# Half-width streams in the doubling of a delta rule's inverse

## The reference, cut to what matters

```python
def step(S, inp):
    q_t, k_t, v_t, g_t, b_t = inp
    Sk = jnp.einsum('bhkv,bhk->bhv', S, k_t)
    delta = jnp.einsum('bhv,bhk->bhkv', v_t, k_t) - jnp.einsum('bhv,bhk->bhkv', Sk, k_t)
    S = jnp.exp(g_t)[..., None, None] * S + b_t[..., None, None] * delta
    o_t = jnp.einsum('bhkv,bhk->bhv', S, q_t)
    return (S, o_t)
_, o = jax.lax.scan(step, S0, xs)
```

## Time and profile before

| | us |
|---|---|
| median of 3 runs | 5181.56 |
| lowest and highest | 5180.79, 5186.57 |
| the profiled execution | 5157.29 |
| span of its trace, first to last instruction | 5155.5 |

### The profile page before, as it was taken

One profiled execution on the slowest core, in us unless ns is written; L12 is line 12 of the kernel. 1 busy time (PEld: TensorE's weight loads), 2 busy tenths in 40 slices (PEclk: granted clock), 3 DMA queues, 4 the chain that ended last, 5 costly groups with the idle time before them and its releaser, 6 DMA issues. The chain is left out here.

```text
span 5155.5 us, 162507 instructions
## 1 busy us (share of the span) xinstructions
PE 4638.3 (90%) x67085; PEld 2981.7 (58%) x67085; DVE 3206.6 (62%) x5639; ACT 2103.2 (41%) x2965; POOL 1162.3 (23%) x1361
## 2 busy tenths in 40 slices
PE   6877869999999999999976666999999999999998
PEld 6333349999999999997644443344444444444443
DVE  4888864444444444443334445787877878787876
ACT  1566632222222222221332221565655656565654
POOL 1355533232323232321014445000000000000000
PEclk9989989999999999999987776999999999999999
DMA  3322221111111111112232224000000000000000
GB/s 103 132 98 98 91 100 51 54 51 54 51 54 46 58 45 60 42 53 63 77 116 63 60 63 99 8 9 12 9 12 8 14 17 4 17 4 17 10 12 8
DMA packets 201355, 250.09 MB, mean 49 GB/s; under 512 B 52865, under 2 KB 132865, under 8 KB 199969
## 3 DMA queue, kind: packets, MB, share of 16 engines
q1 hardware_dynamic: 180240, 209.29, 13.0%
q0 software_dynamic: 6144, 16.79, 1.1%
q10 hardware_dynamic: 14352, 14.55, 0.8%
HBM read 135.18 MB, written 105.38 MB: 47 GB/s over the span
## 5 line engine op out<-in xcount | busy, mean ns | idle before, releaser
L2096 DVE TENSOR_REDUCE part_max<-p_m 128x1 f32<-128x512 f32 x2118 | 1364.0, 686 | 379.6 <-PE p_m L1938 372.1
L2078 ACT ACTIVATE prob<-p_s 128x1024 f32<-128x1024 f32 x1024 | 1047.7, 1023 | 750.4 <-PE p_s L2002 748.5
L1957 PE MATMUL p_o<-prob,v_one 128*64 128x512 f32 x4096 | 1054.3, 592 | 3.9 <-ACT prob L2078 0.5
L1938 PE MATMUL p_m<-keys,queries 96*64 96x512 f16 x4236 | 661.5, 387 | 27.5 <-DMA keys<-parts_d 19.9
L2002 PE MATMUL p_s<-queries,keys 97*64 97x512 f16 x4096 | 619.2, 380 | 1.2 <-issue 0.6
L2002 PEld LDWEIGHTS p_s<-queries,keys 97*64 97x64 f16 x4096 | 227.9, 109 | 600.7 <-issue 594.3
L544 PE MATMUL p_proj<-xn_t_all,proj_w_sb 128*128 (+1 forms) x768 | 389.2, 649 | 78.7 <-ACT raw L570 70.5
L1050 DVE TENSOR_TENSOR inv<-inv,pd_pre 128x512 f32<-128x512 f32 x256 | 176.1, 688 | 406.7 <-PE pd_pre L795 406.7
L962 ACT ACTIVATE inv_low<-pd_low 128x512 f32<-128x512 f32 x320 | 191.0, 597 | 579.4 <-PE pd_low L833 528.3
L1938 PEld LDWEIGHTS p_m<-keys,queries 96*64 96x64 f16 x4236 | 239.3, 108 | 310.5 <-DVE part_max L2096 56.4
L1906 POOL TENSOR_TENSOR attn<-o_num,o_inv 32x512 f32<-32x512 f32 x64 | 81.0, 1265 | 1452.5 <-DVE o_inv L2115 1446.1
(11 more groups left out here) (240 smaller groups left out, 6624.5 us busy)
## 6 DMA issues: line engine op xcount, KB each, us to landing
k_d<-qkv SPq DMA_DIRECT2D x8, 2048.0 KB, 7.5
q_d<-qkv SPq DMA_DIRECT2D x8, 2048.0 KB, 12.3
v_d<-qkv SPq DMA_DIRECT2D x8, 2048.0 KB, 7.3
sums<-sums_d SPq DMA_DIRECT2D x128, 128.0 KB, 3.0
k_t<-k_d SPq DMA_DIRECT2D x64, 256.0 KB, 3.3
q_t<-q_d SPq DMA_DIRECT2D x64, 256.0 KB, 3.4
v_t<-v_d SPq DMA_DIRECT2D x64, 256.0 KB, 4.8
slots_d<-zero ACTq DMA_DIRECT2D x1, 10112.0 KB, 31.9
```

The costliest lines, as they stand in the source:

```text
L1938: last = te.matmul(p_m[k % 2][x * HALF:(x + 1) * HALF, :], queries[0:ROW, p, hh, at:at + HALF], keys[0:ROW, 2 * p + hh, kb * BLK:(kb + 1) ...
L1957: product = te.matmul(p_o[64 * hh:64 * hh + VW, :], g.v_one[:, j, p, hh:hh + 2, :].rearrange("p a d -> p (a d)"), prob[:, j % 2, hh, :], s ...
L2078: a.activation(prob[:, j % 2], p_s[j % 2][:], ACT.Exp, scale=SCORE_SCALE).then_inc(exp_d, 1)
L2096: v.tensor_reduce(part_max[:, hh * SUB + sub, kb:kb + 1], p_m[k % 2][:], AX.X, ALU.max).then_inc(red_d, 1)
```

## The change

In levels 1 to 4 a matrix that is block diagonal with blocks of width 2w is made out of one with blocks of width w. Of the columns of a head only half can change: in `p_low` and `inv_low` the first w of each 2w, in `inv` the second w of each 2w. The changed kernel streams only these 32 of the 64 columns of a head, as a strided view with runs of w = 2, 4, 8 and 16 columns at k = 1 to 4 (at k = 5, for `half`, one run of 32):

```diff
+    def firsts(ap, k):
+        return ap.rearrange("q n (b s w) -> q n b s w", s=2, w=1 << k)[:, :, :, 0, :]
+    def seconds(ap, k):
+        return ap.rearrange("q n (b s w) -> q n b s w", s=2, w=1 << k)[:, :, :, 1, :]
+    def of_head(part, buffer, hs, p, k):
+        return part(buffer[hs, p:p + 1, :], k).rearrange("q n b w -> q (n b) w")
         def half(n, x, k):
-            each(p_pre[x], of(upper[x]), of(inv_low[x])).then_inc(half_d[x], 1)
+            for p, hs in heads():
+                last = te.matmul(of_head(firsts, p_pre[x], hs, p, k), upper[x][hs, p, :], of_head(firsts, inv_low[x], hs, p, k), start=True, stop=True)
+            last.then_inc(half_d[x], 1)
         def low(n, x, k):
-                last = te.matmul(p_low[x][hs, p, :], inv[x][hs, p, :], step[x][hs, p, :], start=False, stop=k == NL - 1, skip_group_check=True)
+                last = te.matmul(of_head(firsts, p_low[x], hs, p, k), inv[x][hs, p, :], of_head(firsts, step[x], hs, p, k),
+                                 start=False, stop=k == NL - 1, skip_group_check=True)
         def up(n, x, k):
             if k == NL:
                 wait_apart(pe, g, (step_d[x], n.level[k]))
-            each(p_pre[x], of(step[x]), of(inv[x])).then_inc(upmm_d[x], 1)
+                last = each(p_pre[x], of(step[x]), of(inv[x]))
+            else:
+                for p, hs in heads():
+                    last = te.matmul(of_head(seconds, p_pre[x], hs, p, k), step[x][hs, p, :], of_head(seconds, inv[x], hs, p, k),
+                                     start=True, stop=True)
+            last.then_inc(upmm_d[x], 1)
         def keep_low(n, x, k):
-            a.activation(inv_low[x][:], p_low[x][:], ACT.Copy).then_inc(lowc_d[x], 1)
+            if k == 0:
+                a.activation(inv_low[x][:], p_low[x][:], ACT.Copy).then_inc(lowc_d[x], 1)
+            else:
+                a.activation(firsts(inv_low[x][:], k), firsts(p_low[x][:], k), ACT.Copy).then_inc(lowc_d[x], 1)
         def add_up(n, x, k):
-            v.tensor_tensor(inv[x][:] if k < NL else inv_fin[:, n.ring[x]], inv[x][:], p_pre[x][:], ALU.add).then_inc(up_d[x], 1)
+            if k < NL:
+                v.tensor_tensor(seconds(inv[x][:], k), seconds(inv[x][:], k), seconds(p_pre[x][:], k), ALU.add).then_inc(up_d[x], 1)
+            else:
+                v.tensor_tensor(inv_fin[:, n.ring[x]], inv[x][:], p_pre[x][:], ALU.add).then_inc(up_d[x], 1)
```

## The result

| | before | after |
|---|---|---|
| median, us (4 runs each) | 5182.28 | 5267.10 |
| lowest and highest | 5180.79, 5186.57 | 5228.49, 5275.96 |
| the profiled execution | 5157.29 | 5266.16 |
| its span and mean granted clock | 5155.5, 0.951 | 5264.4, 0.929 |

The changed kernel is slower: the ratio is 1.0148, its 95% interval 1.0097 to 1.0198. The forecast was faster, 5148 us. The time lies inside the range of 5065 to 5290, on the side of its rivals.

The account below looks back on a forecast made before the run. TensorE's stream, paced by 64-column weight loads, was taken to bound the delta phase. 832 groups x 0.04 us gave 33 us off 5157.3, 5124 us profiled; scaled to the runs 5148 us, range 5065 to 5290.

Parts of the forecast that it names:

- The pace of a group: TensorE, delta phase: loads of 64 columns set each group's step, with matmuls no longer than the load lying beside them.
- The naive 389 us: TensorE's 832 changed groups: saving of 0.47 us each if streamed columns set the pace; chance 0.06.
- The gain of 33 us: TensorE's 832 changed groups: 0.04 us off each, from 0.935 to 0.895 us.
- The 0.08 us between 0.855 and 0.935: A group's excess over half its lower-clock time; it might stay (0 us) or go entirely (67 us over 832 groups).
- main case's upper end: Delta phase load-bound with full clock, chance 0.58, between -67 and 0 us; at this end nothing is gained.
- ScalarE and VectorE at nothing: `keep_low` and `add_up`: 55 us less ScalarE and 70 us less VectorE work, costed at zero under TensorE's stream.
- The clock stays, 0.58: TensorE's granted clock stays full through the load-bound delta phase; chance 0.58, around -33 us.
- The rival, held at 0.20: TensorE's clock falls in the delta phase, 0.8 us per slow group; one in five gives 5282 us; chance 0.20.
- The strided stream, 0.12: Strided reads and PSUM writes slow changed groups: 82 us slower if only runs of two, 350 if all; chance 0.12.
- The floor per matmul, 0.04: A minimum time per matmul limits changed groups: from 0.935 to 0.80 us, 112 us gained, 5070 us; chance 0.04.
- TensorE's own stream alone bounds the phase, the stops are fixed: Delta phase as long as TensorE's stream; mid-group stops mostly unchanged, perhaps taking a third of the 33 us.
- The phase's end at 2384 us: The delta phase was taken to run from 728 to 2384 us.

Follow-up runs that it names:

- e_cols48: The changed kernel with the first 48 columns of a head streamed contiguously in the changed groups, not computing the inverse; ratio 0.9990.
- e_half_only: The changed kernel with `low` and `up` back at 64 streamed columns, only `half` streaming 32; ratio 0.9996.
- e1_engines_only: The kernel before with only the narrowed `keep_low` and `add_up` on ScalarE and VectorE, TensorE's products untouched; ratio 0.9991.
- e_last_both: Kernel before with narrowed ScalarE and VectorE work, level 5 of `half` and `up` at 32 loaded and streamed columns, `add_up` there split; ratio 1.0192.
- e_cols32: The changed kernel with the first 32 columns of a head streamed contiguously instead of the strided view, not computing the inverse; ratio 1.0201.
- e_both32: The changed kernel with 32 loaded and 32 contiguous streamed columns in the changed groups, not computing the inverse; ratio 0.9981.

## Why the prediction was wrong

**The pace of a group: right.** "With 64 columns of weights the load sets the step." 16, 32, 48 and 64 streamed columns give 0.93 us, 32 loaded columns give 0.89 and 0.52. The naive 389 us did not come. The steps of 0.107 and 0.105 us, read at the lower level in two different phases, had pointed to it.

**The gain of 33 us: over-sized, by the term of 0.04 us a group.** The 0.08 us between 0.855 and 0.935 stayed nearly whole; the group measures 0.93. It is the main case's upper end, "they stay: 0 us". In e_cols48 and e_half_only, where the clock holds, the gain is 0.1% and 0.04%, neither clear of zero. By the medians after is 85 us slower, less than the 110 us that its clock costs. Of the 25 us between, 12 are stops with no releaser: 60 us in the phase of after, 72 in that of e1_engines_only. A slow stretch takes fewer instructions in the same time and can make up for them. Whether the rest is a part of the gain is open.

**ScalarE and VectorE at nothing: right**, by e1_engines_only.

**The clock stays, 0.58: this step failed.** The rival, held at 0.20, came, and its price of 0.8 us a group measures 1.71 - 0.93 = 0.78. That 5267 us lies so near its 5282 is luck in part: it took one group in five, 166, at the lower level and 33 us of gain, and no row said how many. The 242 us more at that level are the time of 142 groups, and the gain didn't come. The arguments for it were in the rows already: a busy TensorE at the lower level with 16 streamed columns. What I held against it was that the clock had never fallen with the stops in the phase, and that 22 of 48 groups and `project` stay full. The first says nothing about narrow groups, since it was seen with full ones. The second is an average over a couple, where the narrow groups lie together; e_half_only, where they don't, keeps its clock. The Trainium skill ("TensorE: Matmul & The Clock Gate", section "HAM oscillation — how this bites in real kernels") tells of the clock falling where TensorE idles while it waits for data. The falls of e_last_both agree with it. The rows of after show the clock fall with TensorE busy for 7.37 of 8 us and never idle for more than 0.63, so that reading for idle gaps alone would have missed it.

**The strided stream, 0.12: refuted.** e_cols32 without stride is no faster than after, and runs of 2 to 16 columns leave a group at 0.93. The rule of the Trainium skill that any non-contiguous pattern in PSUM slows matmuls ("Advanced Engine Details and Errata", section PSUM Cachelines) is not seen here, at least not behind loads of this length; whether it would be in a group bound by its stream no run tested.

**The floor per matmul, 0.04: refuted.** Cut to 16 columns the group keeps its 0.93, and in e_both32 32 records take 0.52 us, 16 ns apart on average. That is below the 25 ns that the Trainium skill states ("TensorE: Matmul & The Clock Gate", section "Wait — 56ns, not 53.3ns?"). The records go to two quarters of the array in turn, and on each quarter they are 0.52 / 16 = 32 ns apart, so the figure may still hold for one quarter; over all 32 records of a group, as the estimate of 0.80 us took it, it doesn't.

**TensorE's own stream alone bounds the phase, the stops are fixed: too simple.** It made no difference to this change, but for one that does shorten the groups it would have been the next error: the supply of instructions limits the phase to about what the loads do, and with the clock took back nearly all of e_both32's gain. I had allowed it a third.

**The phase's end at 2384 us: misread.** The last matmul of the phase ends at 2413 us in before; what lies between are the last couple's state and output. It changes no term of the sum.

## What to carry over

Before cutting what TensorE streams, ask whether the load of the stationary operand isn't as long: read group starts, not record durations, at one level of the clock. If it is, fewer streamed columns gain nothing and can cost the clock, above all where the narrow matmuls follow each other without full ones between; cut the loads with them, or better the number of calls. After any such cut read the granted clock and the stops without a releaser first, since both can take the gain back with no wait in the list that names an engine. The clock can fall in two ways, with the engine busy on narrow streams (after) and with the engine waiting (e_last_both), so look at what the engine did before a fall.

## What the runs showed of the hardware

- The granted clock fell with TensorE and its loads busy. At an unchanged pace of 16 calls in 0.93 us, the time at the lower level in the phase was 7, 20, 249 (or 288 contiguous) and 1361 us for 64, 48, 32 and 16 streamed columns. With the loads cut and the streams full it was 10 us. In e_last_both, with full streams in all but 128 groups, it fell in or just behind waits of about 3 us, 23 times.
- For float32 of 64 rows, on two quarters of the array in turn, 16 calls take the longer of the load (0.93 us for 64 columns) and the stream (0.89 us for 64 columns); 0.52 us with 32 of both. All this is at the full clock.
- TensorE's instructions came in one 16-KB packet, 251 matmul and load records, every 4.17 to 4.22 us, in kernels whose groups were as much as 1.8 times apart in speed. A kernel of small matmuls can be bound by that. It shows as stops of up to 3 us without a releaser, 97 of 107 of which ended 1.1 to 1.7 us after a packet landed (e_both32).
